# Fused loop of a graph kernel: the left one-hot of a portion is built behind the weighting of the values

## The reference, cut to what matters

```
q = xn @ Wq.T / SCALING;  k = xn @ Wk.T;  v = xn @ Wv.T      # 8 heads of 32
attn = einsum('ehd,ehd->eh', k[src], q[dst]) + edge_attr   # one score per link and head
a = exp(attn - segment_max(attn, dst));  a = a / segment_sum(a, dst)
x = x + segment_sum(v[src] * a, dst) @ Wo.T
```

## Time and profile before

| | |
|---|---|
| median of three runs | 3696.05 us |
| profiled execution: time, span | 3699.77, 3698.3 us |
| VectorE busy, whole span | 2230.6 us (60%) |
| TensorE busy, whole span | 2921.7 us (79%) |
| left one-hot L2567: 72 of 128 x 2560 and 12 of 128 x 1024 | 202.9 + 14.6 us, 2818 and 1218 ns each |
| weighting L2599: 116 | 272.4 us, 2349 ns each; idle before them 36.0 us |
| exponential L2461: 116 | 27.2 us, 235 ns each |

### The profile page before, as it was taken

The page is one execution under the profiler, slowest core; times in us unless marked ns, Lnnn a source line. Parts: engine busy times, 40 slices in busy tenths (PEclk is TensorE's granted clock), DMA queues, the critical chain, the costliest instruction groups (busy, mean ns, idle before and its releaser), DMA issues. The chain is left out here.

```text
span 3698.3 us, 51548 instructions
## 1 busy us (share of the span) xinstructions
PE 2921.7 (79%) x15453; PEld 2475.1 (67%) x15453; DVE 2230.6 (60%) x3768; ACT 1422.6 (38%) x3858; POOL 1559.4 (42%) x1502
## 2 busy tenths in 40 slices
PE   6247878887878866556855999999899968999797
PEld 4137767776667754434644777777689858999586
DVE  6669999999999977563433233221567673324443
ACT  4036666666666620121212343333355520000221
POOL 4756666666666667534434777000000000112333
PEclk9569999999999988768987999999999989999899
DMA  4588888888888888733446221000134314443433
GB/s 161 163 268 284 288 290 290 292 288 291 290 290 293 290 297 247 231 116 88 69 88 205 19 1 1 1 1 1 43 118 136 114 41 173 154 163 114 126 64 52
DMA packets 293981, 595.31 MB, mean 161 GB/s; under 512 B 81932, under 2 KB 196112, under 8 KB 286832
## 3 DMA queue, kind: packets, MB, share of 16 engines
q0 software_dynamic: 123216, 301.79, 29.8%
q1 hardware_dynamic: 151392, 239.22, 18.6%
q10 hardware_dynamic: 19264, 52.97, 4.6%
HBM read 432.10 MB, written 164.34 MB: 161 GB/s over the span
## 5 line engine op out<-in xcount | busy, mean ns | idle before, releaser
L2415 POOL DMA_INDIRECT gnn_got<-kv,gnn_edge x928 | 877.8, 946 | 421.3 <-issue 266.0
L2525 PE MATMUL gnn_p_out<-gnn_got,gnn_ident 128*128 128x264 f32 x1856 | 475.7, 414 | 0.0
L2525 PEld LDWEIGHTS gnn_p_out<-gnn_got,gnn_ident 128*128 128x128 f32 x1856 | 386.6, 208 | 76.9
L2503 PE MATMUL gnn_p_unit<-gnn_spread,gnn_hot 128*128 128x100 f32 x3072 | 366.1, 279 | 87.1 <-ACT gnn_spread L2432 85.7
L2503 PEld LDWEIGHTS gnn_p_unit<-gnn_spread,gnn_hot 128*128 128x128 f32 x3072 | 356.2, 194 | 113.8 <-issue 110.5
L2432 ACT ACTIVATE gnn_spread<-gnn_spread,gnn_w_of 128x50 f32<-128x50 f32 x1536 | 357.5, 322 | 134.5 <-DVE gnn_spread L2571 134.5
L510 ACT ACTIVATE ffn_h<-ffn_pA,ffn_hb,ffn_hs 128x384 f32<-128x384 f32 (+1 forms) x320 | 197.0, 617 | 344.8 <-PE ffn_pA L579 344.8
L1204 PE MATMUL ffn_pA<-hw,slabs 128*128 128x256 f32 x1250 | 308.5, 410 | 2.2 <-POOLq L1069 2.2
L1204 PEld LDWEIGHTS ffn_pA<-hw,slabs 128*128 128x128 f32 x1250 | 302.4, 336 | 5.3 <-POOLq L1069 2.6
L2489 PE MATMUL gnn_p_body<-gnn_q,gnn_scaled 128*128 128x264 f32 x236 | 95.0, 490 | 261.0 <-DVE gnn_got L2599 206.8
L2599 DVE TENSOR_TENSOR gnn_got<-gnn_got,gnn_p_body 128x2112 f32<-128x2112 f32 x116 | 272.4, 2349 | 36.0 <-ACT gnn_p_body L2461 36.0
(11 more groups left out here) (454 smaller groups left out, 4928.0 us busy)
## 6 DMA issues: line engine op xcount, KB each, us to landing
slabs<-weight_table SPq DMA_DIRECT2D x25, 1600.0 KB, 6.8
weight_table<-gnn_weight_half SPq DMA_DIRECT2D x24, 1600.0 KB, 9.1
count_table<-gnn_count_row SPq DMA_DIRECT2D x12, 3200.0 KB, 18.2
gnn_cell<-count_table ACTq DMA_DIRECT2D x50, 576.0 KB, 3.8
gnn_q<-order SPq DMA_DIRECT2D x120, 132.0 KB, 4.1
state<-gnn_out SPq DMA_DIRECT2D x116, 136.0 KB, 3.6
ffn_xs<-by_expert SPq DMA_DIRECT2D x60, 260.0 KB, 3.3
gnn_got<-kv,gnn_edge POOLq DMA_INDIRECT x928, 3.9
```

The costliest lines, as they stand in the source:

```text
L2415: pool.indirect_dma_start(out=got[k][:, r, :], out_offset=None, in_=kv_dram, in_offset=rows_at(edge[k][:, r, 0:1])).then_inc(gathered[k], 16)
L2503: last = nc.tensor.matmul(p_unit[c % BANKS_OF][:, r * 2 * BOTH:(r + 1) * 2 * BOTH], hot[j % 2][:, at, :], spread[j % 2][:, at, :], start=T ...
L2525: nc.tensor.matmul(p_out[k % 2][:, 0:MSG], ident[:], got[k][:, r, MSG:2 * MSG], start=(r == 0), stop=False)
```

## The change

In VectorE's `run`, the call of `fill_hot` (one wait and one instruction) stands behind the weighting instead of ahead of the wait for the exponential. Nothing else is changed.

```
                     if j == 0:
                         dve.wait_ge(slots_turned, i + 1)
                         dve.tensor_copy(w_of[:], weight_of).then_inc(w_copied, 1)
-                    if j is not None and j < len(PORTIONS):
-                        fill_hot(i, j)
                     dve.wait_ge(weights_ready[k], g)
                     dve.tensor_tensor(values, values, over(weights, [P, R, HEADS, HD + 1], "p (r h a) -> p r h a", h=HEADS, a=1),
                                       ALU.mult).then_inc(msg_ready[k], 1)
+                    if j is not None and j < len(PORTIONS):
+                        fill_hot(i, j)
                     dve.wait_ge(out_ready[k - 1], g if k == 0 else g + 1)
                     dve.tensor_tensor(faded[v][:].rearrange("p (h d) -> p h d", h=HEADS),
```

## The result

The changed kernel takes 3751.66 us in the median of three runs (3749.36 to 3755.02), against 3696.05 before: the medians lie 55.6 us apart, where 53.9 were forecast. The ratio estimated from the runs is 1.0143, with a 95% interval of 1.0129 to 1.0156, which stands for 48 to 58 us. The profiled execution is the one of 3749.36 us, with a span of 3747.8: 49.5 us longer than the one before.

A forecast was written before the change was run, and what follows sets the result against it. VectorE was taken to set the pace in the pairs, GpSimd's gathers behind them. 28.5 + 30.0 - 4.6 = +53.9 us on the median 3696.05 gave 3750 us, range 3745 to 3756, or 3738 to 3760 with rivals 1 and 3.

The forecast's parts named there:

- (a): Bodies j = 1 to 6 of all pairs and j = 0 of the first: 0.39 us more in each of 73, 28.5 us.
- (b): Bodies j = 0 of pairs 1 to 11: the late exponential stays put, the one-hot adds 2.73 us each, 30.0 us.
- (c): Inside the pairs: the delay hides VectorE's waits for gathers, -4.6 us.
- (d): Behind the last pair: nothing changes; GpSimd's last long stall and the loop's end shift with the end of the pairs.
- The row that was to support (b): First body behind the pairs, without a one-hot: its weighting's 4.76 us wait read as 1.86 + 2.73 and some 0.2.
- the clock's term: TensorE in portion bodies: two waits become one of 2.7 us, which does not bring the clock down; nothing added.
- the 4.6 to 4.8: Sign: the weighting's wait in us after the change, at eleven j = 0 and the first body behind the pairs.
- long matmuls in portion bodies: Sign on TensorE that the forecast is wrong: matmuls in portion bodies show the long durations.
- Rival 2: TensorE's longer idle stretch drops its clock; alternating bodies would add 58 us, giving 3808 us; chance 0.04.

The follow-up runs named there:

- number 2: Kernel before with the left one-hot behind the weighting at j = 1 to 6 alone: 3727.60 us against 3699.57.
- Number 5: Changed kernel with the right one-hot moved into the wait for the exponential, the left one still behind the weighting: 3715.06 us against 3698.44 for the kernel before.
- Number 1: Kernel before with the left one-hot behind the weighting at j = 0 alone: 3721.70 us against 3699.57.
- number 4: Changed kernel with ScalarE's last four copies of turned units behind the next pair's j = 0 exponential: 3704.20 us against 3699.57 for the kernel before.
- number 3: Changed kernel with 12 identity matmuls on TensorE ahead of each portion's products: 3772.46 us against 3699.57 for the kernel before.
- number 9: Changed kernel with the load of j = 0 issued ahead of the previous pair's big stores: 3754.05 us against 3703.86 for the kernel before.
- numbers 6 and 7: Kernel before, at j = 0: both one-hots ahead of the wait, 3699.43 us; ScalarE's last four copies behind the exponential, 3681.59 us; each against 3698.44.
- number 8: Changed kernel with 12 identity matmuls on TensorE ahead of each portion's products, except portion 6: 3747.95 us against 3698.44 for the kernel before.

## Why the prediction was right

The two large terms of its sum were right, and so was their mechanism. That the total came within 2 us of the medians is in part luck: two smaller terms were wrong by about as much in opposite directions. Point by point, by its steps.

- **(a) 0.39 us in 73 bodies, 28.5 us.** Measured 12.12 - 11.72 = 0.40 in the body shown, and undisturbed pairs longer by 92.64 - 90.32 = 2.32 us with j = 1 to 6 alone (number 2), where 6 x 0.39 = 2.34. Only j = 0 of the first pair, the 73rd, costs about 0.2, since the small copy stands in its wait. The neighbouring body without a portion gave the right price for an order that the trace did not have. Number 5 shows the cause: with 1.1 us of other work in the wait the 0.39 go away.
- **(b) 2.73 us at eleven j = 0, 30.0 us.** The wait rose from 1.86 to 4.60 us. Number 1 has pairs longer by 2.73 us, and number 4 gives 51 us back by taking the copies out of the way. The chain that makes the exponential late was named rightly: number 3, which lengthened it, made j = 0 worse by 2.0 us.
- **(c) 4.6 us of waits for gathers go.** They went, and more with them. The pairs of the kernel before take 1088.8 us; undisturbed they would take 88.38 for the first and 11 x 90.32, 6.9 us less. Of these, 4.8 are waits for gathers, and 1.4 are one longer wait at j = 0 of the seventh pair (3.25 us instead of 1.86), behind products of portion 5 that took 6.33 us; the rest is small. None of it is left after the change. Number 1 shows it by itself: its pairs took 23.3 us more, which is 30.2 less 6.9.
- **(d) Nothing changes behind the pairs.** The part got 3.1 us shorter. GpSimd's last long stall ended 1348.85 - 1314.74 = 34.1 us after the pairs; after the change it is 1401.71 - 1370.75 = 31.0. From there to the last fade it takes 171.0 and 171.1 us. So the end does hang on that stall, as the prediction says, but the stall doesn't end a fixed time after the pairs. The shorter wait in the first of these bodies (below) may be why; no run shows that. The other half of the step holds: GpSimd's stalls on these loads went up from 148.3 to 190.5 us, number 9 took them down to 126.0, and the pairs' period stayed. In the changed kernel they are time in hand; in the kernel before hardly any of it was left (numbers 6 and 7).

```profile
1401.71 0.94 POOL L2415 DMA_INDIRECT gnn_got<-kv,gnn_edge  x1 [13.02 <-DMA gnn_q<-order]
```

- **The sum.** With TensorE's wait filled (number 8) the pairs take 1140.3 - 1088.8 = 51.4 us more than before; with the 6.9 us that went this makes 58.3, where (a) and (b) have 58.5. The clock, which the prediction put at nothing, adds 2.2. So (c) was 2.3 us too small and the clock's term 2.2 us too small, and the two cancel: the pairs became 53.7 us longer. Over the whole span the two profiled executions differ by 49.5 us and the medians by 55.6, so no agreement closer than a few us means anything.
- **The row that was to support (b) was misread.** The 4.76 us of the first body behind the pairs were read as 1.86 + 2.73 + 0.2. After, the same body waits 3.38 (the row below), not the 4.6 to 4.8 that the prediction named. This body has no table load (there are twelve, the last at 1233.0 us before), so a wait like that of the other pairs would be 4.6 - 1.28 = 3.3. In the kernel before the products of portion 5 in the last pair had run in part at the low clock, 6.33 us for 40 matmuls instead of 4.70, and the exponential behind them was 1.4 us late, as in the seventh pair. Two errors met in one number.

```profile
1379.51 2.35 DVE L2597 TENSOR_TENSOR gnn_got<-gnn_got,gnn_p_body 128x2112 f32<-128x2112 f32 x1 [3.38 <-ACT gnn_p_body L2461]
```

- **The clock.** The prediction said, from the earlier trace rows, that one wait of 2.7 us does not bring TensorE's clock down, and it named long matmuls in portion bodies as a sign of being wrong. That sign is there. Of the 72 sets of 40 products after, 46 took 4.70 us, 16 took 6.33 and ten 7.8 to 8.0; all 24 that came after an idle time of 2.9 us or more are among the long ones. TensorE after, in a stretch where the bodies alternate:

```profile
664.24 4.70 PE L2503 MATMUL gnn_p_unit<-gnn_spread,gnn_hot 128*128 128x100 f32 x40 [1.31 <-ACT gnn_spread L2432]
...
676.35 6.33 PE L2503 MATMUL gnn_p_unit<-gnn_spread,gnn_hot 128*128 128x100 f32 x40 [2.94 <-ACT gnn_spread L2432]
...
688.47 4.70 PE L2503 MATMUL gnn_p_unit<-gnn_spread,gnn_hot 128*128 128x100 f32 x40 [1.31 <-ACT gnn_spread L2432]
```

After 2.94 us of idle time the products take 6.33 us, so that the next wait is only 1.31 us, and after that they take 4.70. The granted clock is 0.76 from 676 to 683 us, so partly the level of 1.2 GHz, and 1.00 from 688 to 693, the level of 2.4. Rival 2 had this pattern, alternating bodies, but priced it at 58 us, as if TensorE had no time in hand. It has: the long products end late, ScalarE reads them late, and the exponential still finds ScalarE ready in nearly all bodies (ten portion bodies have waits of 0.49 to 0.64 us instead of 0.30). In the windows the granted clock of such stretches fell:

```profile
240.00:300.00 60.00, 49.92 (x297) 44.97 (x297) 57.13 (x40) 41.40 (x170) 45.37 (x48) 0.91 0.83 239
```

It was 0.98 in the same stretch before; with TensorE's wait filled (number 8) it is 1.00, and the products take 4.71 us:

```profile
240.00:300.00 60.00, 59.24 (x422) 55.30 (x422) 57.38 (x41) 41.36 (x170) 45.38 (x49) 1.00 0.83 237
```

The page of the Trainium skill that was weighed (TensorE: Matmul & The Clock Gate, section "HAM oscillation — how this bites in real kernels") says that a loop with waits between its matmuls can fall to the low clock anew in each iteration. This trace agrees in part: the clock falls and comes back again and again, but the products are long in 26 of the 72 bodies and not in each. On the time it hardly bears, since TensorE was not the engine that the loop waits for: 2.2 us in the pairs by number 8.

What stays open: why the last stall behind the pairs ended 3.1 us earlier, and what makes two executions differ by some us outside the loop.

## What to carry to other kernels

Work that an engine does between handing something over and needing it back is not only work: it covers the partner's answer, and here moving it behind the wait cost the smaller of the two, the work or the wait that it left empty, in every round: 0.39 of 2.73 us where the partner answers at once, 2.73 whole where it is 4.6 us late. To price such a move, look for a round of the same loop that lacks the work, and read its wait; then look for the rounds in which the partner is late, for there the whole piece comes out. And before gaining time on the engine that sets the pace, look at how far the next limit is: here the last third of a per cent, 11 to 12 us, was to be had only after the loads were moved as well.

## What was not expected of the hardware

TensorE's clock falls in this loop also without a long wait: in the kernel before the products that start at 1301.85 took 6.33 us after an idle time of only 1.49 us, while most of the bodies like it took 4.70.

```profile
1301.85 6.33 PE L2503 MATMUL gnn_p_unit<-gnn_spread,gnn_hot 128*128 128x100 f32 x40 [1.49 <-ACT gnn_spread L2432]
```

And in number 2 six sets of products took 4.70 us after an idle time of 2.8 to 3.0 us, where all such sets of the changed kernel were long. The same idle time so goes with either duration, and the rows could not tell which it would be.
